# The last stage of a two-layer graph network, run inside the engine programs of the stage before it

## The reference, cut to what matters

```python
h = layer_norm(x, ln1_w)
xl, xr = h @ lin_l_w.T + lin_l_b, h @ lin_r_w.T + lin_r_b
z = leaky_relu(xl[src] + xr[dst] + edge_attr @ lin_edge_w.T, 0.2)
logits = einsum('ehc,hc->eh', z, att)
alpha = softmax of logits over the edges of each dst
attn_out = segment_sum(xl[src] * alpha, dst) + attn_bias
x = x + attn_out
h2 = layer_norm(x, ln2_w)
x = x + relu(h2 @ fc_w.T) @ proj_w.T          # fc_w 512x128, proj_w 128x512
# and outside the layer
out = layernorm(x1 + x)
```

## Time and profile before

| | |
|---|---|
| median of 3 runs | 2989.43 us (2985.38 to 2994.2) |
| the profiled execution | 2994.84 us, span 2993.0 us |
| TensorE matmul busy | 2201.2 us, 74% of the span |
| GpSimd busy | 1725.0 us, 58% |
| VectorE busy | 1718.3 us, 57% |
| ScalarE busy | 1126.6 us, 38% |
| mean granted TensorE clock | 0.826 of 2.4 GHz |

### The profile page before, as it was taken

How to read it: one execution, slowest core, us unless ns; L and a number is a source line. 1 busy time by engine, 2 the same in 40 slices (tenths; PEclk the granted TensorE clock), 3 DMA queues, 4 the chain that set the end, 5 groups by cost and what they waited for, 6 DMA issues and landing times. The chain is left out here.

```text
span 2993.0 us, 52671 instructions
## 1 busy us (share of the span) xinstructions
PE 2201.2 (74%) x14461; PEld 1756.5 (59%) x14461; DVE 1718.3 (57%) x7092; ACT 1126.6 (38%) x2973; POOL 1725.0 (58%) x1739
## 2 busy tenths in 40 slices
PE   7766665666666666667578888887888887888779
PEld 5665665665555666556355555555555665656556
DVE  2355555555555555557346656666666666666766
ACT  2355555555555555555333222222222222222123
POOL 3356666666666666655565656666666666666322
PEclk9687788788788877887788888987888888888879
DMA  5344444444444444432644444444444444444201
GB/s 136 97 117 111 109 112 105 113 113 109 109 111 114 106 112 112 123 88 59 171 148 141 147 142 126 144 143 140 144 146 147 144 131 139 146 146 147 62 20 36
DMA packets 378501, 356.41 MB, mean 119 GB/s; under 512 B 61695, under 2 KB 335743, under 8 KB 371424
## 3 DMA queue, kind: packets, MB, share of 16 engines
q1 hardware_dynamic: 314640, 236.51, 28.3%
q0 software_dynamic: 53248, 109.16, 14.2%
q10 hardware_dynamic: 10320, 7.37, 0.9%
HBM read 338.98 MB, written 13.82 MB: 118 GB/s over the span
## 5 line engine op out<-in xcount | busy, mean ns | idle before, releaser
L846 POOL DMA_INDIRECT rows<-xl_tab,src_cols x832 | 844.0, 1014 | 505.9 <-issue 228.1
L279 POOL DMA_INDIRECT rows<-in_x,src_cols x832 | 796.6, 957 | 537.0 <-issue 208.9
L330 PE MATMUL tile_sums<-gather,rows 128*128 128x128 f32 x1664 | 420.1, 342 | 254.4 <-DVE node_sums L560 172.4
L560 DVE TENSOR_TENSOR node_sums<-node_sums,tile_sums 128x256 f32 x832 | 350.0, 421 | 387.1 <-PE tile_sums L332 182.9
L330 PEld LDWEIGHTS tile_sums<-gather,rows 128*128 128x128 f32 x1664 | 322.9, 241 | 296.7 <-issue 190.1
L320 PE MATMUL p_dst<-window,spread 128*128 128x129 f32 x1664 | 331.1, 333 | 200.9 <-issue 154.1
L1022 DVE SCALAR_TENSOR_TENSOR node_sums<-node_sums,shrunk,tile_sums 128x128 f32 x832 | 280.7, 337 | 238.2 <-remote 175.6
L320 PEld LDWEIGHTS p_dst<-window,spread 128*128 128x128 f32 x1664 | 283.6, 241 | 219.8 <-issue 207.6
L332 PE MATMUL tile_sums<-gather,ones 128*128 128x128 f32 x1664 | 389.8, 323 | 0.0
L548 DVE CUSTOM_DVE_ANT_0 product<-rows,p_dst 128x128 f32<-128x128 f32 x832 | 258.2, 348 | 226.3 <-remote 147.7
L909 PEld LDWEIGHTS z_ps<-spread,window 128*128 128x128 f32 x1664 | 254.6, 221 | 155.2 <-issue 132.9
(11 more groups left out here) (187 smaller groups left out, 2525.7 us busy)
## 6 DMA issues: line engine op xcount, KB each, us to landing
window<-p_tab SPq DMA_DIRECT2D x832, 64.5 KB
attr<-in_attrT SPq DMA_DIRECT2D x52, 1024.0 KB
window<-xr_tab SPq DMA_DIRECT2D x832, 64.0 KB
rel_bc<-rel_rows SPq DMA_DIRECT2D x208, 128.0 KB
rel_bc<-rel_rows SPq DMA_DIRECT2D x52, 512.0 KB
rows<-in_x,src_cols POOLq DMA_INDIRECT x832
rows<-xl_tab,src_cols POOLq DMA_INDIRECT x832
p_tab<-p_rows ACTq DMA_DIRECT2D x13, 258.0 KB, 3.5
```

What stands on the lines that cost most here:

```text
L279: nc.gpsimd.indirect_dma_start(out=rows[:, r, i, :], out_offset=None, in_=t["x"], in_offset=bass.IndirectOffsetOnAxis(ap=src_cols[:, tile: ...
L330: nc.tensor.matmul(tile_sums[k][:, i, 0, :], rows[:, Q % AHEAD0, 2 * k + i, :], gather1[:, Q % 2, 2 * k + i, :], start=True, stop=True)
L560: nc.vector.tensor_tensor(span, span, tile_sums[i // 2][:, i % 2, :, :], ALU.add).then_inc(added, 1)
L846: nc.gpsimd.indirect_dma_start(out=rows[:, r, i, :], out_offset=None, in_=xl_tab, in_offset=bass.IndirectOffsetOnAxis(ap=src_cols[:, tile: ...
```

## The change

The MLP stage disappears as a block of its own. Its functions move into layer 1's engine programs, and the loops there run on to `MLP + node_groups` with `MLP = quads + 2` = 210: step Q carries node block b = Q - 210. So steps 208 to 218, which were only the tail of layer 1, now also carry MLP work, and steps 219 on carry MLP work alone.

- The weights are loaded by SyncE right behind the last window transfer. `fc` is scaled by VectorE at the end of step 207. GpSimd's sums follow its last gather; they wait for `x1_normed`, `message_made` and `z_ready`.
- No SBUF or PSUM is new but for weights and statistics: `hidden` lies on `attr`, `x2` and `mlp_sum` (formerly `total`) on `z_act`, `u` and `result` on `window`, `x1_bias` and `hT` on `rows`, `x12` on `spread`. `a_ps` and `y_ps` become one bank, `ay_ps` (formerly z_ps0), `t_ps` is z_ps1, and there are two `f_ps` banks (the two of `lg_ps`) for four expands.
- `turn_sums(b)` waits for `added` to reach `tiles_before(b)`, and, for the shared bank, for `total_ready` b-2; `contract(b)` waits for `x2_made` of block b+2. Expand k waits for the relu two before it. On TensorE turn_sums(b+2) now stands between expand 1 and expand 2 of block b; before, it stood behind all four.
- In VectorE's step the MLP part stands behind the quad's add_tile, messages and one-hots, in the old order: attend(b+1) (formerly residual), norm1(b-2), norm0(b+1), add_mlp(b-1).
- ScalarE's step has its softmax part first, then copy_hT(b), root(b+1, 0), relu(b), root(b-1, 1).

```diff
+    MLP = quads + 2
...
+        hidden = attr[:].rearrange("p i (k q) -> p i k q", k=FC)
+        x2 = z_act[:, 0].rearrange("p i (t d) -> p i t d", t=QT)
+        mlp_sum = z_act[:, 1].rearrange("p i (t d) -> p i t d", t=QT)
+        u = window[:, 0:2]
+        result = window[:, 2:4]
+        x1_bias = rows[:, 0:2]
+        hT = rows[:, 2].rearrange("p i d -> p (i d)")
+        x12 = spread[:].rearrange("p i (t d) -> p i t d", t=QT)
...
+        ay_ps = z_ps[0][:].rearrange("p (i d) -> p i d", i=QT)
+        t_ps = z_ps[1]
+        f_ps = [bank[:].rearrange("p i d -> p (i d)") for bank in lg_ps]
...
             @block.sync
+                sp.dma_start(a_bias[:], t["attn_bias"].to_broadcast([P, P])).then_inc(mlp_in, DMA)
...
+                sp.dma_start(proj[:], t["proj_wT"].rearrange("(k p) d -> p k d", p=P)).then_inc(mlp_in, DMA)
+                for b in range(node_groups):
+                    sp.wait_ge(result_ready, b + 1)
+                    sp.dma_start(out_dram[b], result[:, b % 2]).then_inc(out_stored[b % 2], DMA)
...
             @block.gpsimd
+                pool.wait_ge(x1_normed, blocks)
+                pool.wait_ge(message_made, quads - ROWS + 3)
+                pool.wait_ge(z_ready, quads)
+                for T in range(quads, MLP + node_groups):
+                    b = T - MLP
+                    if 0 <= b + 2 < node_groups:
+                        bias(b + 2)
+                    if 0 <= b + 1 < node_groups:
+                        residual(b + 1)
...
             @block.scalar
-                for Q in range(quads + LAG):
+                for Q in range(MLP + node_groups + 1):
...
+                    b = Q - MLP
+                    if 0 <= b < node_groups:
+                        copy_hT(b)
+                    if 0 <= b + 1 < node_groups:
+                        root(b + 1, 0)
+                    if 0 <= b < node_groups:
+                        relu(b)
+                    if 0 <= b - 1 < node_groups:
+                        root(b - 1, 1)
...
             @block.tensor
+                def turn_sums(b):
+                    pe.wait_ge(added, tiles_before(b))
+                    if b:
+                        pe.wait_ge(x2_made, b)
+                    if b >= 3:
+                        pe.wait_ge(total_ready, b - 2)
...
+                def expand(b, k):
+                    pe.wait_ge(hT_ready, b + 1)
+                    if b or k >= 2:
+                        pe.wait_ge(relu_ready, FC * b + k - 1)
+                    nc.tensor.matmul(f_ps[k % 2], fc[:, k * P:(k + 1) * P], hT, start=True, stop=True).then_inc(fc_ready, 1)
+
+                def contract(b):
+                    pe.wait_ge(relu_ready, FC * (b + 1))
+                    pe.wait_ge(x2_made, min(b + 3, node_groups))
...
-                for Q in range(quads + LAG + 1):
+                for Q in range(MLP + node_groups + 1):
...
-                    if Q >= LAG + 1:
+                    if 0 <= Q - LAG - 1 < quads:
                         add_up(Q - LAG - 1)
+                    b = Q - MLP
+                    if Q == quads:
+                        pe.wait_ge(mlp_in, 5 * DMA)
+                        pe.wait_ge(fc_scaled, 1)
+                        pe.wait_ge(z_split, quads)
+                    if Q == MLP:
+                        pe.wait_ge(lowered, groups)
+                    if 0 <= b < node_groups:
+                        turn_u(b)
+                    if 0 <= b - 1 < node_groups:
+                        contract(b - 1)
+                    if 0 <= b < node_groups:
+                        expand(b, 0)
+                        expand(b, 1)
+                    if 0 <= b + 2 < node_groups:
+                        turn_sums(b + 2)
+                    if 0 <= b < node_groups:
+                        expand(b, 2)
+                        expand(b, 3)
...
             @block.vector
-                for Q in range(quads + LAG + 2):
+                for Q in range(MLP + node_groups + 2):
...
+                    b = Q - MLP
+                    if Q == quads - 1:
+                        dve.wait_ge(mlp_in, 5 * DMA)
+                        nc.vector.tensor_scalar(fc[:], fc[:], ln2_col[:, 0:1], None, ALU.mult).then_inc(fc_scaled, 1)
+                    if 0 <= b + 1 < node_groups:
+                        attend(b + 1)
+                    if 0 <= b - 2 < node_groups:
+                        norm1(b - 2)
+                    if 0 <= b + 1 < node_groups:
+                        norm0(b + 1)
+                    if 0 <= b - 1 < node_groups:
+                        add_mlp(b - 1)
```

More of the change, by code:

```diff
@@ L697, in build @@
     ROWS = 16
+    FC = 4
+    MLP = quads + 2
     AHEAD = 4
@@ L873, in keep_shrunk, with root, copy_hT, relu @@
                     nc.scalar.copy(shrunk[:, s % 2], shares_ps).then_inc(shrunk_made, 1)
+                def root(b, k):
+                    act.wait_ge(var_ready[k], b + 1)
+                    nc.scalar.activation(std[:, k, :], mv[:, k, :, 1], ACT.Sqrt,
+                                         bias=eps_cols[:, 0:1]).then_inc(std_ready[k], 1)
+                def copy_hT(b):
+                    act.wait_ge(turned, b + 1)
+                    if b:
+                        act.wait_ge(fc_ready, FC * b)
+                    nc.scalar.copy(hT, t_ps[:]).then_inc(hT_ready, 1)
+                def relu(b):
+                    if b >= 2:
+                        act.wait_ge(y_ready, b - 1)
+                    for k in range(FC):
+                        act.wait_ge(fc_ready, FC * b + k + 1)
+                        nc.scalar.activation(hidden[:, b % 2, k, :], f_ps[k % 2], ACT.Relu).then_inc(relu_ready, 1)
                 def norm_x1(b):
@@ new lines, in link, with moments @@
+                def link(ins):
+                    n[0] += 1
+                    ins.then_inc(step, 1)
+                    dve.wait_ge(step, n[0])
+                def moments(k, src):
+                    for i in range(QT):
+                        ins = nc.vector.bn_stats(stats[:, k, i, :], src[:, i, :])
+                    link(ins)
+                    for i in range(QT):
+                        ins = nc.vector.bn_aggr(mv[:, k, i, :], stats[:, k, i, :])
+                    ins.then_inc(var_ready[k], 1)
@@ new lines, in norm0, with add_mlp @@
+                def norm0(b):
+                    if b >= 2:
+                        dve.wait_ge(turned, b - 1)
+                    scaled(b, 0, u[:, b % 2], x2[:, b % 2]).then_inc(u_ready, 1)
+                def add_mlp(b):
+                    dve.wait_ge(y_ready, b + 1)
+                    dve.wait_ge(x12_ready, b + 1)
+                    nc.vector.tensor_tensor(mlp_sum[:, b % 2], ay_ps, x12[:, b % 2], ALU.add).then_inc(total_ready, 1)
+                    dve.wait_ge(total_ready, b + 1)
+                    moments(1, mlp_sum[:, b % 2])
@@ L986, in make_spread, with norm1 @@
+                def norm1(b):
+                    if b >= 2:
+                        dve.wait_ge(out_stored[b % 2], b // 2 * DMA)
+                    scaled(b, 1, result[:, b % 2], mlp_sum[:, b % 2]).then_inc(result_ready, 1)
                 def make_spread(Q):
@@ L1204, in _ @@
                     A = Q - LAG - 2
-                    adds = A >= 0
+                    adds = 0 <= A < quads
                     if adds:
```

265 lines of the change are left out of this document (85 added, 180 removed).

## The result

The changed kernel takes 2974.49 us in the median of 15 runs (2959.16 to 2988.68), the kernel before 2989.43 us in the median of 15. The ratio is 0.9948, with a 95% interval of 0.9931 to 0.9965: 15.5 us faster by the ratio (14.9 by the medians), where 14.3 (to 2975) was forecast.

What follows compares the result with a forecast made beforehand. VectorE bounds layer 1's drain, nobody works in the stretch after it, TensorE bounds the MLP. Walking the overlapped steps gave a span of 2978.7 us, 14.3 less; off the median 2989.4 that makes 2975, range 2968 to 2986.

Steps and rivals of the forecast that it cites:

- VectorE's wait ahead of the last pick_grown: Step 211: spread_shares and keep_shrunk stand behind the MLP work in their queues, so VectorE waits 3 us.
- a shared step: Steps 213 to 216, drain plus MLP work on VectorE: 3.08 + 6.45 + 0.15 for y_ps = 9.7 us.
- The structure: Drain laid over seven to nine of thirteen MLP steps, empty stretch gone, then TensorE-bound steps of 8.40 us.
- (c): Rival: attend(0) begins only when the drain ends; 8.1 us gained, 5.7 given back, 2987 us; chance 0.08.
- The relu wait: In TensorE-bound steps contract waits 0.67 us for the last relu; a step becomes 8.40 us, 0.44 more.
- The two f_ps banks: Expand 2 waits for relu 0: nothing, bound 0.67 us a step if turn_sums is late.
- The register load: window_bases behind the chained moments in drain steps: 0.2 us a step (0 to 0.35), 0.8 over four steps.
- GpSimd's biases: Nothing: GpSimd's queue is empty after the last gather, two tensor ops some 2.5 us of a 10 us step.
- The clock fall: TensorE idles 3 us in step 212 and its clock falls once: 2 us added, range 0 to 4.
- (b): Rival: merged steps couple tighter over one shared bank, 1 to 1.5 us more a step; 2982 to 2986; chance 0.15.
- (d): Rival: TensorE's clock stays low through shared steps, 18.5 us each instead of 9.7; 3001 with three; chance 0.07.
- ScalarE's tables: Exp and Sqrt alternate, three loads of 1.28 us more, each in idle ScalarE time: nothing, bound 3.9 us.

Runs made afterwards that it cites:

- run without overlap: Changed kernel with MLP = quads + 12, so attend(0) stands in step 219 behind layer 1's whole tail: tail 159.4 us, time ratio to before 0.998.
- split wait: Changed kernel with contract starting on three relus and waiting for the fourth only in front of its fourth product: tail 143.4 us.
- own bank: Changed kernel with turn_sums, from block 6 on, writing the bank of ends_ps and standing behind all four expands: tail 144.8 us.
- two near kernels: Changed kernel with turn_sums in its own bank from block 6 (tail 144.8 us), or with add_tile's register load ahead of the MLP part (146.4 us).

## Why the prediction was right

Point by point, in the order of its sum (times from the start of the tail, which the prediction's own times reach by taking off 2829.98):

| | forecast | measured |
|---|---|---|
| x2 of block 0 | 7.3 | 7.3 |
| x2 of block 1 | 16.2 | 15.5 |
| x2 of block 2 | 23.8 | 22.9 |
| VectorE's wait ahead of the last pick_grown | 3 | 2.75 |
| x2 of block 4 (48.9 with one clock fall, 46.9 without) | 48.9 | 45.7; 47.3 with the fall |
| a shared step | 9.7 + 0.2 | 9.99 |
| from x2 of block 7 to the end of turn_sums(12) | 41.2 | 41.3 |
| from there to the end | 28.7 | 29.1 |
| tail | 148.7 | 146.1; 147.7 with the fall |
| lost just ahead of the tail, beside the biases | 0 | 1.8 (0.9 to 2.4 in other profiles) |

- **The structure** held: empty stretch gone, drain under VectorE-bound steps, then a TensorE-bound part that runs 0.44 us a block slower than before. The shared step is less VectorE's alone than the prediction had it: VectorE works 8.9 of its 10 us and not 9.5 of 9.7, and mlp_sum waits for a contract that itself waited for x2. (VectorE's part of a step was added up as 6.45 us; its rows give 4.38 + 2.01 = 6.39.) The run without overlap shows the split: 3.6 us without it, 13.3 with it. By the same run the prediction's (c) was well priced (8.1 gained and 5.7 given back; measured 8.5 and 2.1 gained, 4.4 and 2.6 given back).
- **The relu wait** behind the last expand was rightly named as the 0.44 us: the split wait takes it away, and steps go to 7.9.
- **The two f_ps banks** were priced at nothing because turn_sums stands between; in the own bank run, which took it from there, the four expands took 0.2 us more.
- **The register load** was mis-sized: taken as 0.2 us a shared step, it is 0.33, just inside its bound of 0.35.
- **GpSimd's biases** were priced at nothing, since its queue is empty then. It is, but beside them VectorE's one-hots of step 206 took 2.51 us instead of 0.86, and 1.8 us went ahead of the tail. The term was mis-sized.
- **The clock fall** was 2 us in the sum for step 212; it costs 1.6 when it comes. That it stayed away in the profile after is 2.0 of the 2.6 us by which that tail was shorter than forecast; the first steps were 1.2 shorter (norm0 among them, 1.52 instead of 1.84 us), the shared steps and the end 0.6 longer.
- **The median** came within 0.5 us of the forecast, closer than the working, and that part is luck: the tail was 2.6 us shorter than forecast, the 1.8 us ahead of it were not in the sum, and the two nearly cancel (15.2 us off in the profiles, 14.3 forecast). Executions of the changed kernel differ by up to 30 us, of which its three tails show 1.6.
- **Rivals.** (b), tighter coupling, is real but small: the own bank's shared step was 0.3 us less, where (b) had 1 to 1.5. (c) is the run without overlap, which is not what the change does. (d), the low clock through the shared steps, did not come: in the changed kernel the clock was 1.00 from x2 of block 4 to that of block 7 and 0.99 behind it. The Trainium skill, "TensorE: Matmul & The Clock Gate", section "HAM oscillation", has idle gaps put the array back to the low clock. The traces agree in direction; but 3.02 us of idle time came with a fall in one profile of the changed kernel and not in two others.
- **ScalarE's tables**: the prediction had three loads more; there are two more (three in the tail instead of one). Each was over before its user was due, so nothing. The drain that the Trainium skill, "ScalarE: Activation LUTs", section "What ACT_TABLE_LOAD costs", adds to each switch is not to be seen in these rows.

## What to carry to other kernels

When a stage is laid beside the tail of another, the gain is the covered part of the tail plus the removed block end, less what the shared banks and the new order cost in every later step; here 16.9 us were 3.6 for the block end (after 7 us given back) and 13.3 for the cover, and some 1.8 of them were lost again just ahead of the stretch that I measured, where work moved forward on an idle engine slowed a busy one. So begin the stretch ahead of the first instruction that moved. Then read which engine bounds each side, add its two rows for the shared step, and look at what moved out from between a producer and its consumer: 0.44 us of other work had hidden a relu. A wait on only the part of an input that the first instructions need gives such a cover back for one moved line.

## What was not expected of the hardware

- A tail that repeats within 0.1 us on chips that differ by 15% in the whole kernel (the changed kernel's span is 2972.7 us on one and 2517.2 on another, with a tail of 146.07 and 146.09): the difference lies in the stages ahead of it. Only the fall of the clock moved it, to 147.7.
- The same program with the same 3.02 us of idle TensorE kept its clock in two profiles and lost it in a third, for 1.6 us; with two near kernels and the split wait counted in, it was lost in three of six.
- A small VectorE operation (pick_grown, 0.18 us) took 1.27 us when it started beside a GpSimd tensor_tensor of 1.27 us, and ended with it. Norm0's four operations took 1.84 us beside a GpSimd bias and 1.52 us where they overlapped one in part; the one-hots' four took 2.51 us beside two biases, 0.86 alone.
